# Dense filler products in the opening of a four-layer transformer kernel, and a new instruction order for all engines

## The reference

```python
ada = (c @ W_ada + b_ada)[:, None, :]
shift1, scale1, gate1, shift2, scale2, gate2 = jnp.split(ada, 6, axis=-1)
h = _layernorm(x) * (1.0 + scale1) + shift1
Q = (h @ Wq + bq).reshape(B, N, NHEAD, HEAD_DIM)      # K, V likewise
scores = jnp.einsum('bqhd,bkhd->bhqk', Q, K) / np.sqrt(HEAD_DIM).astype(np.float32)
attn = jax.nn.softmax(scores, axis=-1)
attn_out = jnp.einsum('bhqk,bkhd->bqhd', attn, V).reshape(B, N, D_MODEL) @ Wo + bo
x = x + gate1 * attn_out
h = _layernorm(x) * (1.0 + scale2) + shift2
return x + gate2 * (jax.nn.gelu(h @ W1 + b1, approximate=False) @ W2 + b2)
```

## Time and profile before

| | |
|---|---|
| median of 3 runs | 376.62 us (376.16 to 376.84) |
| the profiled execution | 376.23 us, of which the traced span is 374.2 us |
| VectorE, ScalarE busy | 326.6 and 316.0 us |
| TensorE, GpSimd busy | 361.1 and 186.7 us |
| first maximum; first `EXP` product | 20.28 us; 34.20 us |

### The profile page before, as it was taken

How to read it: one execution, slowest core, us unless ns; L and a number is a source line. 1 busy time by engine, 2 the same in 40 slices (tenths; PEclk the granted TensorE clock), 3 DMA queues, 4 the chain that set the end, 5 groups by cost and what they waited for, 6 DMA issues and landing times.

```text
span 374.2 us, 10210 instructions
## 1 busy us (share of the span) xinstructions
PE 361.1 (97%) x3649; PEld 203.8 (54%) x3650; DVE 326.6 (87%) x768; ACT 316.0 (84%) x632; POOL 186.7 (50%) x290
## 2 busy tenths in 40 slices
PE   8789899999999999999999999999999999999987
PEld 3513444546645555555556555464545565456876
DVE  6486999999999989899999899999999999963663
ACT  6302687999999899899899899999989999998774
POOL 5334899956488213785024582205861031104774
PEclk9855999999999999999999999999999999999999
DMA  7710246321003200006000024000042000000001
GB/s 249 214 39 16 56 109 167 108 80 35 0 3 102 73 3 0 6 4 170 4 3 5 2 59 114 4 2 4 3 111 63 3 1 3 3 3 4 3 0 56
DMA packets 17185, 17.62 MB, mean 47 GB/s; under 512 B 2460, under 2 KB 15454, under 8 KB 17120
## 3 DMA queue, kind: packets, MB, share of 16 engines
q1 hardware_dynamic: 15840, 16.19, 15.7%
q10 hardware_dynamic: 1296, 0.79, 0.8%
HBM read 6.62 MB, written 0.52 MB: 19 GB/s over the span
## 4 chain that ended last, share of the span: by engine, by line
PE 63%; DVE 7%; POOL 3%; ACT 3%; issue 2%; ACTq 0%; POOLq 0%
PE pv_ps L830 19%; PE max_ps L645 10%; PE exp_ps L654 10%; PE max_ps L777 7%; PE exp_ps L764 6%; DVE mx L1129 5%; PE exp_ps L620 2%; PE exp_ps L699 2%; PE max_ps L620 2%; PE max_ps L635 2%; ACT probs L955 1%; PE exp_ps L815 1%; POOL rstd L1150 1%; PE max_ps L735 1%; PE exp_ps L635 1%
## 5 line engine op out<-in xcount | busy, mean ns | idle before, releaser
L1129 DVE TENSOR_REDUCE mx<-max_ps 128x1 f32<-128x512 f32 x384 | 240.1, 681 | 9.9 <-PE max_ps L645 8.7
L955 ACT ACTIVATE probs<-exp_ps 128x512 f32<-128x512 f32 x384 | 201.0, 604 | 11.8 <-PE exp_ps L654 10.9
L645 PE MATMUL max_ps<-k_stack,q_stack 64*128 64x512 bf16 x384 | 112.2, 394 | 4.6 <-DMA k_stack<-parts 3.4
L830 PE MATMUL pv_ps<-probs,v_ones 128*32 128x256 f32 x1536 | 103.1, 385 | 0.0
L654 PE MATMUL exp_ps<-q_stack,k_stack 64*128 64x256 bf16 x768 | 99.8, 273 | 0.0
L1149 POOL TENSOR_SCALAR var_eps<-mv 128x2 f32<-128x2 f32 (+2 forms) x33 | 6.4, 193 | 144.9 <-DVE mv L989 144.3
L830 PEld LDWEIGHTS pv_ps<-probs,v_ones 128*32 128x32 f32 x1536 | 43.4, 109 | 32.3 <-issue 8.8
L645 PEld LDWEIGHTS max_ps<-k_stack,q_stack 64*128 64x128 bf16 x384 | 31.7, 94 | 49.6 <-DVE mx L1129 29.2
L654 PEld LDWEIGHTS exp_ps<-q_stack,k_stack 64*128 64x128 bf16 x768 | 41.5, 95 | 29.0 <-ACT probs L955 12.5
L967 ACT ACTIVATE mrows<-exp_ps 8x256 bf16<-8x256 bf16 x48 | 17.4, 363 | 13.4 <-PE exp_ps L815 13.3
L764 PE MATMUL exp_ps<-hT,w 128*128 128x256 f32 x96 | 26.7, 396 | 0.0
(11 more groups left out here) (126 smaller groups left out, 471.1 us busy)
## 6 DMA issues: line engine op xcount, KB each, us to landing
k_stack<-parts SPq DMA_DIRECT2D x36, 128.0 KB, 2.4
q_stack<-parts SPq DMA_DIRECT2D x30, 128.0 KB
w<-in_w_dram SPq DMA_DIRECT2D x4, 448.0 KB, 3.8
w<-in_w_dram SPq DMA_DIRECT2D x4, 256.0 KB, 3.0
w<-in_ada_dram SPq DMA_DIRECT2D x1, 896.0 KB, 4.8
w<-in_rows_dram SPq DMA_DIRECT2D x1, 832.0 KB, 6.7
q_stack<-mrows SPq DMA_DIRECT2D x48, 4.0 KB
x<-in_x_dram SPq DMA_DIRECT2D x2, 256.0 KB, 3.3
```

Source lines behind the costliest of these rows:

```text
L645: return pe.matmul(max_bank(n), half(q_stack, b, pair, j)[:, t * P:(t + 1) * P], half(k_stack, b, pair, j), start=True, stop=True)
L830: mm = pe.matmul(pv_ps[32 * j:32 * j + 32, cols_of(g // 2)], v_ones[:, b, kt, 4 * g + j, :], probs[:, (4 * i + j) % RING_P, cols_of(of_two ...
L955: act.activation(probs[:, tile % RING_P, :], exp_bank(e), ACT.Exp, scale=SCORE_SCALE[hc // 2 // NB]).then_inc(exp_read, 1)
L1129: dve.tensor_reduce(mx[:, G % 2, t, 2 * (pair % 2) + j:2 * (pair % 2) + j + 1], max_bank(n), AX_X, ALU.max, negate=True).then_inc(max_read, 1)
```

## The change

Four things change. `ADA1` gets 14 more products of the zero tile ahead of its waits (`FIRST_PRODUCTS[3]`). The four `WARM` items (eight products) are gone. Each of the 14 `MAX` items that stand before the first `EXP` is followed by three products of `k_stack` that nothing reads (`product_beside`): for the first eleven (`ACCOMPANIED`) they alternate between the two halves, beginning with the other one, half 1 into the bank that `V` of chain 0 had used and half 0 into `pv_ps`; for the last three all are in half 0. `take_exp` waits for all fillers before that bank is used again. And `ORDER_TEXT` is another string with the same items (less `w`); in VectorE's stream the first two maxima of each group from the third group on also wait for the split two groups back (`max_split`).

```diff
-FIRST_PRODUCTS = [16, 2, 4]
+FIRST_PRODUCTS = [16, 2, 4, 14]
 EARLY_GATES = 1
-WARM_BEATS = 4
+BESIDE_PRODUCTS = 3
...
 ORDER_TEXT = """
-mnmnnmmnmSnmnRmntwnmyAwSmEEnErEwnmtwnREEmytEEEnmPEmEnntSmmEEnRVEmDnEntEmnEmEDSPnmEEnEPRmmSEDEEnAnmtPRnDEmEnEPEmEmnEEmESPnEDmEnER
...
+tmnAnmmtynytnmStnmnRtmmnEEmnnEEmDEEnSEVmmEnRAnmmSPnEmEnPRnEDEEmnEmEEnPSmEmtnDEEPnREmEEmnmESEPnEDmEnERPmnEEnEEmmrEPSEnEmnEPmORDED
...
+NEXT_IN_V_BANK = EXP_USE["V", 0, WHOLE, 0] + EXP_BANKS
+def maxima_before(wanted):
+
+    return [item for item in ORDER[:next(n for n, item in enumerate(ORDER) if wanted(item))] if item[0] == "MAX"]
+ACCOMPANIED = maxima_before(lambda item: EXP_USE.get(item) == NEXT_IN_V_BANK)
+BEFORE_EXP = maxima_before(lambda item: item[0] == "EXP")
...
             def take_exp(n):
 
+                if n == NEXT_IN_V_BANK:
+                    pe.wait_ge(beside_done, len(ACCOMPANIED) * BESIDE_PRODUCTS)
                 if n >= EXP_BANKS:
...
+            def product_beside(j):
+
+                pe.wait_ge(*read_by_act(("V", 0, WHOLE, 0)))
+                out = exp_bank(EXP_USE["V", 0, WHOLE, 0]) if j == 1 else pv_ps[:, :]
+                pe.matmul(out, half(k_stack, 0, 0, j)[:, 0:P], half(k_stack, 0, 0, j), start=True, stop=True).then_inc(beside_done, 1)
...
                 elif name == "ADA1":
                     n = MAX_USE[item]
+                    first_products(FIRST_PRODUCTS[3])
                     pe.wait_ge(ada1_in, 32)
...
-                if name == "WARM":
-                    for _ in range(2):
-                        pe.matmul(pv_ps[:, :], k_stack[:, 0, 0, 0:P], k_stack[:, 0, 0, :], start=True, stop=True)
-                elif name == "EXP":
+                if name == "EXP":
...
                     score_for_max(hc, m, j).then_inc(max_full, 1)
+                    if item in BEFORE_EXP:
+                        for filler in range(BESIDE_PRODUCTS):
+                            product_beside((j if filler % 2 else 1 - j) if item in ACCOMPANIED else 0)
...
                     pair, t = max_pair_of(m)
+                    if G >= 2 and m % GROUP_BEATS == 0:
+                        dve.wait_ge(max_split, G - 1)
                     dve.wait_ge(max_full, FULL[n])
```

More of the change, by code:

```diff
@@ L164, in streams @@
         "D": [item for k in range(1, CHAINS) for item in copies(k)],
-        "t": with_counts(["ST", "XH", "TR", "K", "Q", "SQ"], 1, WHOLE), "w": [("WARM", n, 0, 0) for n in range(WARM_BEATS)],
+        "t": with_counts(["ST", "XH", "TR", "K", "Q", "SQ"], 1, WHOLE),
         "A": [("ANG", b, WHOLE, 0) for b in range(NB)], "r": [("RED", n, WHOLE, 0) for n in range(2 * NB)], "s": [("SIN", 0, WHOLE, 0)],
@@ L172 @@
 ORDER_TEXT = """
-mnmnnmmnmSnmnRmntwnmyAwSmEEnErEwnmtwnREEmytEEEnmPEmEnntSmmEEnRVEmDnEntEmnEmEDSPnmEEnEPRmmSEDEEnAnmtPRnDEmEnEPEmEmnEEmESPnEDmEnER
-DPnEErmnxPOEEmnEESPmEmEnRPmEEnGEEEmPESFEEnmnrPRmEanEEnEmESaEEPRanEmnEEPEmEmEEnPamEnEmEPnOErnEEaSGEmPRmnbamnabaabmbnEEabanEmEnbZb
-ambbSmnSabbsmnRbPPEnmnaaabEmaEnmEbESnmERPRmEEEnnbbbEEEmEnPDmmEnaEEPEnbEmEEDmSPEnEEmnRPDnOEmEDEEGmESPEnDcnDEEmRFccVnEmEPEcmnmESEc
-PnnEmRccnmccnmESEcmnEEEmRPEnEEmnPEEEcmnEPmEncEEPSEnmnEEPmOEmcGRSEEnmcdEncddREEnmdEFmPPnEndmEcSddmncddnmEEdEZEdnmEEPmdEEnRPnEdcEm
@@ L177 @@
[L177 to L180, removed]
@@ L181 @@
-SPEmEnmEPRiEnEEmnPEmnEEEnPSmEnEmEPORmniGimniimEEnSiiRnEmEmEEVjnmEEnEiPEmEnEnEPESmnEiEmRiPmnjiSiFnEmEEnRPmnPEmEmEnjSEPEmEEEnPREmE
-nEmPjnmOEEnEPmESEEGnEmEPREnkjmEnEmEPnEEESPREEkEkEPEEEEiEiEPkEEEFjPiPOkjjjGjqlkkjllqqlkjqkklqjlkqllklqqqjqqljljkqklijqlqkklllqjql
-jlqkjqiijjlkqkiqljqqklqlkklk
+tmnAnmmtynytnmStnmnRtmmnEEmnnEEmDEEnSEVmmEnRAnmmSPnEmEnPRnEDEEmnEmEEnPSmEmtnDEEPnREmEEmnmESEPnEDEmnERPmnEEnEEmmrEPSEnEmnEPmORDED
+nEEEmEnmPSEEnnEmPmEnRnEEEEmGrSPmEEnnEPRErmEnmEamEEPEFxnErmaESEEEnmPREanmEnaPPmnOEEaGZnEEmEEmbanmanbbaamnSbasnambRPnmbbnmbSbmnEaS
@@ new lines @@
+EbaEbnEmnEPRRmEEbnaaaabEmEnEmPEnEmbmEnbmEbbSEEnnEEDmRPEnDmEPSEnEEmnDRPaEmmEEEnPbEmnSEPOEmDEEDEnGEnDmVnmcREmFEnSEPmEEnEEcmERPcEnE
+EmnPmEEEEncPmnEEEmScPnmEnRccmncScnmcEcnEEmnEPcRPmEEnmEcSPOmEnEcGnEmFERcdmEEnEddEmnEEPEdEmnPdmnEEcSddnmcddEnmZSEddEmEEnnRPPdmEnEc
+EmdRPSnmddEEddRnEEmEEPmnEEdEnPEmDSnEPOEEEmEnDGVEmEDnEmDDPnEDEmPSREnEEmnPmnReEmEEeEnEEmmESPnEEmeEnRPEnmeEEEPmEEnPEmSnEemEPORnEEnE
+meGemnPnSmfeefEEfmEEnfemnEfnEeRPmnmffffEmEnefeFfmESEnfEmPeeeefEnEmSRPEnmEZEnfffeRnEEmEmPnnEEEEmSPnmDEEEnVfmEDfRDEnEmPEnEEmnPDDOm
@@ new lines @@
+EEnEESGPmEEDmEnPSREngEmnERgEmEEnEgPmEnEEmPnEEEmSEPEnmEgPFREnEmEnPEmgEnmESPOmEnGgRmnghmnghhgnmhEEgnEmEhEmgPnnmgShhShhEnmEhhgnmRRP
+EEZmnhggggnEmEhEEnmPEnmEhmnhhhEgEmEEnSPEnEmDDDnERSPmEEmEnRPnEEEhDmDmESPEEnmEnPOEEDEmnEGmERPEnEEiSnmEmRPnEmEEEnPnEEmEmEPSnEEEiEmi
+EnRPmEEniEEPmEEnmSEiPnEEEmnRPOmniinmSiinmEEiRmEnEmiEVEnEEnmPEEEmnEPEESnmEmRPnEnEEGEEEmiSPnEEEmnjiPRiEEmmEnEPmEnEEnEPmEmEEnSPOFEE
+mnmRiniGPSEEmnnEPRmEjkEmEEnmEPEnSEEPRjEEEkEEiEjEEEiPEEPEEkjPiPOjkGjjqljkqqllqjkkjkkjqlkqlqkqlllkljqljklqqlkqjjijlqkklqlqjlkjkqqq
@@ L184 @@
+ljkiiljqjliqkjkkqlqkllql
 """
@@ L454, in build @@
         rows_in_stack = [sem(f"rows_in_stack{n}") for n in range(2)]
-        quad_done, quad_out = sem("quad_done"), sem("quad_out")
+        quad_done, quad_out, beside_done = sem("quad_done"), sem("quad_out"), sem("beside_done")
         cond_ready, silu_exp, mod_ready = sem("cond_ready"), sem("silu_exp"), sem("mod_ready")
```

## The result

The changed kernel takes 377.87 us (median of 16 runs, 376.56 to 381.11), the kernel before, on the same chip, 376.62 (median of 16; 374.31 to 377.67, but for one at 544.38): a ratio of 1.0053, 95% interval 1.0029 to 1.0077. A second measurement gave 1.0078 (1.0044 to 1.0112). The change makes the kernel slower, by 0.5 to 0.8%. The forecast was 374.2 us and faster; the time lies outside its range, which ended at 376.9.

The account below looks back on a forecast made before the run. No single engine was taken to set the pace, VectorE being busiest. -3.1 us (opening) + 0.3 (half-array stretches) + 0.4 (`W1` chunk near the end) = -2.4 gave 373.8, as a median 374.2 us; range 371.5 to 376.9.

Parts of the forecast that it names:

- the 2.98 us of the sum: Ahead of `ADA1`: 14 products at 0.213 us spacing take 2.98 us, hidden in TensorE's 3.43 us idle time.
- the cover of 0.45 us: Before the first score: 0.45 us stay idle on TensorE after `GATE` 0; once gone, every 0.1 us shows in full.
- the 19.7: Opening, TensorE: the prediction counts as wrong if the first score starts after 19.7 us.
- I take zero: The 92 added `max_split` waits of maxima on VectorE: already met when reached, so priced at zero.
- the 3.7 us that was the bound: The 92 waits on VectorE: 3.7 us if each cost as much as the unexplained difference in the maxima's spacing.
- the first step: Opening, to the 24th maximum on VectorE: it ends at 40.9 us, before at 44.0, a lead of 3.1 us.
- the second step: Table behind the opening: +0.3 us for more half-array stretches, +0.4 for a `W1` chunk behind the last `PV`.
- plus or minus 2 us around zero: Rest of the table: what the search wins or loses elsewhere, unreadable, put at plus or minus 2 us from idle times.
- rival 3: Behind the opening the new table packs worse: 3 us more VectorE idle time cancels the lead, 4 gives 377.5; chance 0.11.
- its own signs: Wrong if clock 0.5 exceeds 4 us, first score starts after 19.7, or VectorE's or ScalarE's later idle grows over 2 us.
- rival 1: Opening: the clock falls but returns in time; 4 us of low clock cost about 2 us, 376 to 376.6; chance 0.10.
- Rival 2: Opening: the clock stays low through all the scores, first `EXP` near 47 us, loss near 8 us, 384; chance 0.03.

Follow-up runs that it names:

- three comparisons: Waits varied: old order with fillers, 375.82 us with the 92 and 375.93 without; kernel before with the 92, 0.9992; changed kernel with only 44, 1.0051.
- the three pairs of runs: New order against old, alike in fillers: with all fillers 1.0078 against 0.9981, with the 14 alone 1.0038 against 0.9935, with none 1.0082 against 0.9969.

## Why the prediction was wrong

**Right in the main: the opening.** The 14 products take the 2.98 us of the sum. But the clock fell under the gate's products, which end at 19.89 and not 19.21: the cover of 0.45 us was used up, the first score starts at 19.83, past the 19.7 that the prediction gave as a sign of being wrong, and the first maximum at 21.81 and not 21.3. These 0.5 us are most of what the lead lacks at the 24th maximum, 2.4 us for 3.1. The fillers are hidden while the clock holds. Their increments add nothing that shows: fillers that each increment a semaphore start 0.22 us apart, beside a bare spacing of 0.213. The Trainium skill (TensorE: Matmul & The Clock Gate, "The cost: per-tile semaphore tail") says that such increments serialize, at 26.3 ns each; this trace shows no such addition between fillers. `XH` takes 1.11 us, and the first `EXP` product starts at 34.02 (forecast 33.8).

**Right: the waits.** "I take zero" for the 92 waits held, in three comparisons, to within 1.3 us; the 3.7 us that was the bound is excluded.

**Wrong, the first step: the lead of 3.1 us carried whole to the end.** The prediction counted to the 24th maximum "because VectorE is the busiest engine", and let the -3.1 stand undiminished in the sum. Two kernels on the old order lead by 2.4 and 3.3 us there, and neither kept it. The control without `WARM` can be followed item by item, since its order is the old one. At the 24th maximum VectorE leads by 2.4 us; TensorE's first `PV` products lead by 2.2, 40.37 against 42.54, and ScalarE's fifth exponential by 2.1 (its first, 34.19 against 35.26, by only 1.1). So all three engines had the lead. From the 96th maximum on VectorE leads by 1.1, and the last output copy ends at 341.65 instead of 342.71. The loss lies for the most part in three splits of VectorE that meet an operation of GpSimd, take longer and end with it (see the last section): 0.2 us in the third, 0.5 in the fifth and 0.55 in the tenth. The fifth and the tenth split of the control:

```profile
53.33 0.68 DVE L1142 TENSOR_TENSOR mparts<-mx,mparts 128x8 bf16<-128x8 f32 x1
...
83.94 0.79 DVE L1142 TENSOR_TENSOR mparts<-mx,mparts 128x8 bf16<-128x8 f32 x1
```

The same two in the kernel before:

```profile
55.22 0.17 DVE L1123 TENSOR_TENSOR mparts<-mx,mparts 128x8 bf16<-128x8 f32 x1
...
85.64 0.24 DVE L1123 TENSOR_TENSOR mparts<-mx,mparts 128x8 bf16<-128x8 f32 x1
```

The lead is 1.88 us ahead of the fifth and 1.37 behind it; it is 1.70 ahead of the tenth and 1.15 behind it (in between an `xhat` operation wins 0.4 us, with 0.34 for 0.77). A lead shifts each engine against the others by another amount, and operations meet that did not meet before. This is the trace of one execution.

The old order with the 14, the fillers and the waits leads by 3.1 us at the first three output copies and by 1.1 at the last. Two of its steps, 0.7 us each, lie ahead of the fourth and of the tenth copy, and in both TensorE stands still while the profile shows nothing that it waits for ("issue"):

```profile
123.27 0.59 PE L663 MATMUL max_ps<-k_stack,q_stack 64*128 64x512 bf16 x3 [0.68 <-issue]
...
283.00 0.50 PE L663 MATMUL max_ps<-k_stack,q_stack 64*128 64x512 bf16 x2 [0.56 <-issue]
```

Without the waits the same kernel has three, of 1.01, 0.71 and 0.49 us, and its lead of 2.6 us is gone by the tenth copy. Behind 42 us the kernel before, the control and the old order with the 14 have none above 0.3 us. Of the changed kernel's two profiles one has a stand of 1.0 us, the other two, of 0.5 and 1.0. What causes these stands is open.

Nor is the clock the whole of such a lead. The control reaches its 24th maximum 2.4 us early with the clock low for 24 us. What it lacks are the eight `WARM` products, in the table since before, at 0.43 us each at half clock, up to 3.4 us of TensorE in all. But the low clock has a price too: the kernel before, with no edit, has executions with less of it, and these are 2.2 us faster (last section). And the profiled execution of the kernel before with 24 more products, whose clock is low only from 17.6 to 31.2 us, also ends its 24th maximum at 41.6, with `WARM` in place. The two gains don't add up: the old order with the clock held throughout (374.7 and 374.9 us) is hardly faster than the control.

**Wrong, the second step: +0.7 us, with "plus or minus 2 us around zero", for the rest of the table.** Against the old order with the same fillers and waits it costs 2.1 us at a like clock: inside the 2 us that the prediction allowed either way, but three times its 0.7. Where it lies is read from two windows, 42 to 340 us and 340 to 376, which is past the end; TensorE's busy time is the first number behind a window's length. The kernel before:

```profile
42.00:340.00 298.00, 295.25 (x3274) 161.72 (x3277) 281.42 (x634) 278.77 (x555) 144.63 (x221) 1.00 0.15 40
340.00:376.00 36.00, 30.00 (x230) 26.20 (x222) 16.91 (x63) 23.35 (x56) 21.96 (x43) 0.99 0.06 16
```

The changed kernel:

```profile
42.00:340.00 298.00, 292.20 (x3226) 159.97 (x3223) 281.23 (x629) 272.78 (x544) 138.61 (x213) 1.00 0.14 39
340.00:376.00 36.00, 31.43 (x234) 26.39 (x234) 17.18 (x63) 24.34 (x58) 21.30 (x42) 1.00 0.06 16
```

The old order with fillers and waits:

```profile
42.00:340.00 298.00, 294.16 (x3267) 161.50 (x3269) 278.98 (x629) 277.47 (x550) 143.51 (x219) 1.00 0.14 39
340.00:376.00 36.00, 28.92 (x210) 25.57 (x202) 16.70 (x62) 22.28 (x55) 20.88 (x42) 0.97 0.06 16
```

The old order without `WARM` and fillers:

```profile
42.00:340.00 298.00, 294.76 (x3270) 161.37 (x3273) 280.60 (x630) 278.17 (x553) 145.85 (x222) 1.00 0.15 39
340.00:376.00 36.00, 28.97 (x210) 25.65 (x202) 16.72 (x62) 22.34 (x55) 20.99 (x42) 0.98 0.05 15
```

The two busy times of TensorE added are the work that it has left at 42 us; the span less 42 less that sum is its idle time from there on:

| profiled execution | span | work left at 42 us | idle from 42 us on |
|---|---|---|---|
| before | 374.2 | 325.25 | 6.95 |
| old order, no `WARM`, no fillers | 373.2 | 323.73 | 7.47 |
| old order, fillers and waits | 373.1 | 323.08 | 8.02 |
| changed | 375.0 | 323.63 | 9.37 |

The changed kernel has 1.6 us less work left than the one before, and loses 2.4 us in idleness: +0.8. The old order with the same fillers has 2.2 us less left and loses 1.1: -1.1. These are single executions, whose signs agree with the medians, and TensorE's busy time is not pure work, since products of both halves overlap. The new order does pack worse, as the three pairs of runs show: rival 3, held at a chance of 0.11, is the nearest to what happened, though at less than its 3 us of VectorE's idle time, and on TensorE and ScalarE instead. By its own signs, too, the prediction was wrong: ScalarE's idle time behind the opening grew by 5.7 us, where 2 was the limit, and VectorE's hardly (280.50 us busy for 280.65). The terms of the sum, as near as runs come to them (a mean clock of 0.995 or more): fillers and waits on the old order are worth 1.0 us, where the lead was put at 3.1 (375.75 against 376.73), and the new order costs 2.1 for the 0.7 of the sum, of which the ending has 0.7 where 0.4 was forecast. Together +1.1, and the changed kernel's 377.87 is 1.1 above 376.73. The long fall of the clock comes on top.

**Partly right: rival 1.** The clock falls for about 3.5 us in both profiled executions of the changed kernel, and for ten in that of its version with 44 waits. The short fall is cheaper than the 2 us that the rival gave it: the old order with fillers and waits takes 374.7 and 374.9 us at a mean clock of 1.0, and 374.9 to 376.5, in the median 375.9, at 0.995: about one. The long one (380 to 381) wasn't foreseen between rivals 1 and 2, and in the second measurement half of the runs have it: this, not only the table, makes the medians 377.9 and 379.7. Which dip comes is not in the program; the Trainium skill (TensorE: Matmul & The Clock Gate, "What's actually happening") calls the transition "run-variable", and the runs here agree: the two groups lie some 3 us apart. Rival 2's 384 doesn't follow from its own working, in which the first `EXP` comes 12.8 us later than before and the loss is near 8; no execution of the changed kernel had a mean clock below 0.986.

**Open.** What in the new order idles TensorE is not settled by a run. Of the 2.4 us of idle time that the changed kernel's profile has more than the one before, one stand with nothing to wait for is 1.0:

```profile
231.10 0.37 PE L663 MATMUL max_ps<-k_stack,q_stack 64*128 64x512 bf16 x1 [1.01 <-issue]
```

Such stands can't be the order's alone, since the old order with fillers has them as well. Splits that meet GpSimd are a second candidate, untested too.

## What to carry to other kernels

Where several engines run in lockstep through few buffers, an engine that idles 16 of 297 us is not free: 3 us of work added to it, or to the one beside it, cost about 3 us. A lead won in the opening is not carried to the end by itself: in a control with the old order, follow it item by item against the kernel before, and look at what stands where it shrinks. Before crediting a stall to a low clock alone, take out what was put there against it: here eight warming products cost 2.4 us of an engine's lead and about 1.2 us of the time, and leaving them out was worth as much as all of the new fillers. The fastest version of those run is the old order with only the 14 products, 0.9935 (0.9909 to 0.996), whose interval overlaps the control's. A fresh table by a search is a change of its own, to be measured apart from the edit that it came with.

## What the hardware did unexpectedly

**VectorE waits for GpSimd in the middle of a split.** The split's second operation, a subtraction of two operands in SBUF, is usually 0.17 us long. The changed kernel's VectorE and GpSimd at two splits:

```profile
62.91 1.69 POOL L1191 TENSOR_TENSOR wg<-w,gate 128x128 f32<-128x128 f32 x2
63.44 0.15 DVE L1140 TENSOR_REDUCE mparts<-mx 128x8 bf16<-128x8 f32 x1
63.62 1.01 DVE L1142 TENSOR_TENSOR mparts<-mx,mparts 128x8 bf16<-128x8 f32 x1
...
115.96 1.69 POOL L1191 TENSOR_TENSOR wg<-w,gate 128x128 f32<-128x128 f32 x2
116.18 0.15 DVE L1140 TENSOR_REDUCE mparts<-mx 128x8 bf16<-128x8 f32 x1
116.37 1.30 DVE L1142 TENSOR_TENSOR mparts<-mx,mparts 128x8 bf16<-128x8 f32 x1
```

Both end within 0.03 us of GpSimd's pair (63.62 + 1.01 = 64.63 beside 62.91 + 1.69 = 64.60; 117.67 beside 117.65), while the reduction of one operand, just ahead, keeps its 0.15 us under GpSimd too. In the changed kernel 16 of 48 subtractions are longer than 0.3 us, and each ends within 0.03 us of an operation of GpSimd; in the kernel before, 9 of 48. The group's total:

```profile
L1142 DVE TENSOR_TENSOR mparts<-mx,mparts 128x8 bf16<-128x8 f32 x48 | 14.6, 304 | 1.7
```

It was 11.8 us before, at 245 ns each. The Trainium skill (SBUF — State Buffer, "Summary: rules for kernel authors") has the rule: a VectorE operation with two SBUF inputs and a GpSimd operation that reads SBUF exclude each other, and the second to issue blocks. The traces agree to 0.03 us. A table that moves a split beside `wg` can so cost VectorE a microsecond; most of what the control lost of its lead went in this way. It is not the whole account of the changed kernel: `XH` is 1.6 us shorter in the changed kernel, and the new order with only the 14 products has 13.3 us in this group and is slow as well, and the control has 13.3 us and is fast.

**The kernel before has its own spread in the clock.** Where its mean clock is 0.977 to 0.982 it takes 373.9 to 375.8 us (24 executions beside the runs above, median 375.0), at 0.967 to 0.973 mostly 376.5 to 378 (98, median 377.1), with no edit between them. A gain of half a per cent in one execution of a kernel like this can be the clock's.
